# Receptances, output bias and low parts between an MLP and a block-wise mixture of experts: what moves to another engine or another place in the order

## The reference

```python
k = einsum('btd,ed->bte', x * tmk + xs * (1 - tmk), Wk) + bk
v = einsum('btd,ed->bte', x * tmv + xs * (1 - tmv), Wv) + bv
r = einsum('btd,ed->bte', silu(x * tmr + xs * (1 - tmr)), Wr) + br
# scan over t: a = e1 * a + e2 * v, b = e1 * b + e2, wkv = a / b
return einsum('btd,ed->bte', wkv * r, Wo) + bo
```

```python
topw, topi = top_k(softmax(x @ gate_w), 4)      # per token
out = sum over chosen experts of topw * (silu(x @ wg) * (x @ wu)) @ wd
out = out + sigmoid(x @ seg) * ((silu(x @ sg) * (x @ su)) @ sd)
```

## Time and profile before

| | us |
|---|---|
| runs, median (lowest to highest) of 3 | 564.64 (560.38 to 565.92) |
| the profiled execution's own time | 565.75 |
| its span, first to last instruction | 563.9 |
| busy: TensorE, VectorE, ScalarE, POOL | 436.9, 356.6, 271.6, 226.7 |
| TensorE's granted clock, mean over the span (1 is 2.4 GHz) | 0.871 |

### The profile page before, as it was taken

How to read it: one execution, slowest core, us unless ns; L and a number is a source line. 1 busy time by engine, 2 the same in 40 slices (tenths; PEclk the granted TensorE clock), 3 DMA queues, 4 the chain that set the end, 5 groups by cost and what they waited for, 6 DMA issues and landing times.

```text
span 563.9 us, 9855 instructions
## 1 busy us (share of the span) xinstructions
PE 436.9 (77%) x3348; PEld 303.8 (54%) x3348; DVE 356.6 (63%) x858; ACT 271.6 (48%) x518; POOL 226.7 (40%) x301
## 2 busy tenths in 40 slices
PE   1856799999997759788888152497879799999844
PEld 1634455555553348676777141376658566666433
DVE  5595458878873254946548989688673355555336
ACT  7314757767778424141683154352352355655402
POOL 5870224434566430601310254226627135565600
PEclk9956669999999779989799666678989999999958
DMA  7482071111330029600000000299902245444282
GB/s 215 140 147 96 23 99 45 36 36 45 118 102 7 1 80 331 200 1 1 1 1 1 28 28 28 82 230 244 301 29 99 80 111 148 135 140 117 64 309 77
DMA packets 52032, 56.02 MB, mean 99 GB/s; under 512 B 10244, under 2 KB 42893, under 8 KB 51984
## 3 DMA queue, kind: packets, MB, share of 16 engines
q1 hardware_dynamic: 47536, 46.67, 31.1%
q0 software_dynamic: 4448, 8.73, 4.6%
HBM read 35.61 MB, written 21.73 MB: 102 GB/s over the span
## 4 chain that ended last, share of the span: by engine, by line
PE 51%; DVE 22%; ACT 8%; issue 7%; POOL 4%; DMA 4%; SPq 2%; DVEq 0%; ACTq 0%; POOLq 0%
PE ps L2234 7%; PE ps L1971 5%; PE ps L1950 4%; PE ps L2021 4%; PE ps L1929 4%; PE ps L2257 4%; PE ps L2009 3%; PE ps L2215 3%; PE ps L2010 3%; PE ps L2011 3%; PE ps L1983 2%; DVE st L935 2%; ACT probs L1619 2%; DVE h_lo L1102 1%; PE ps L2349 1%
## 5 line engine op out<-in xcount | busy, mean ns | idle before, releaser
L1619 ACT ACTIVATE probs<-ps 128x512 f32<-128x512 f32 x160 | 87.0, 598 | 42.1 <-PE ps L1950 41.4
L1035 DVE TENSOR_REDUCE negm<-ps 128x2 f32<-128x1024 f32 (+1 forms) x64 | 67.6, 1082 | 16.6 <-PE ps L1939 16.1
L843 POOL DMA_INDIRECT y_slots_scratch<-yblk,ids x48 | 47.0, 979 | 50.0 <-issue 29.5
L677 POOL TENSOR_TENSOR rstd<-ve,halfneg 128x4 f32<-128x4 f32 x15 | 16.2, 1079 | 112.5 <-DVE ve L964 46.9
L1929 PE MATMUL ps<-k_all,q_ring 64*128 64x512 f32 (+3 forms) x256 | 51.9, 412 | 7.0 <-DVE negm L1035 4.2
L1971 PE MATMUL ps<-probs,v_all 128*32 128x128 f32 (+3 forms) x512 | 50.9, 474 | 4.8 <-DVE att L1063 3.2
L1950 PE MATMUL ps<-q_ring,k_all 64*128 64x512 f32 (+3 forms) x256 | 42.8, 392 | 14.8 <-ACT probs L1619 13.2
L1659 ACT CAST h_hi<-hf 128x512 fp32r<-128x512 f32 x28 | 17.4, 620 | 65.7 <-DVE hf L1093 63.5
L1950 PEld LDWEIGHTS ps<-q_ring,k_all 64*128 64x128 f32 x256 | 22.4, 201 | 48.7 <-ACT probs L1619 37.6
L1434 DVE COPY xcol<-ps 128x256 f32<-128x256 f32 x48 | 20.4, 424 | 39.2 <-PE ps L2215 39.2
L1038 DVE TENSOR_REDUCE negm<-ps 128x4 f32<-128x1024 f32 (+1 forms) x32 | 30.6, 959 | 21.2 <-PE ps L1939 21.2
(11 more groups left out here) (327 smaller groups left out, 1339.2 us busy)
## 6 DMA issues: line engine op xcount, KB each, us to landing
x_sorted_scratch<-pad SPq DMA_DIRECT2D x6, 1072.0 KB, 12.3
xblk<-x_sorted_scratch SPq DMA_DIRECT2D x96, 67.0 KB
wgu<-in_moe_w SPq DMA_DIRECT2D x4, 1536.0 KB, 17.5
q_ring<-q_parts_scratch SPq DMA_DIRECT2D x64, 64.0 KB
ycomb<-y_slots_scratch SPq DMA_DIRECT2D x8, 512.0 KB, 6.6
wd<-in_moe_w SPq DMA_DIRECT2D x1, 3072.0 KB, 18.4
sraw<-in_moe_w SPq DMA_DIRECT2D x6, 384.0 KB, 3.1
q_parts_scratch<-qparts SPq DMA_DIRECT2D x4, 512.0 KB, 4.5
```

Source lines behind the costliest of these rows:

```text
L843: pool.indirect_dma_start(out=y_slots, out_offset=bass.IndirectOffsetOnAxis(ap=ids[:, i:i + 1], axis=0), in_=yblk[:, i % YR, :], in_offset ...
L1035: dve.tensor_reduce(negm[:, par, :, hp, qt], pair_of, AX.X, ALU.max, negate=True).then_inc(s1_read, 1)
L1619: act.activation(probs[:, par, u, :], ps[:, col_unit(g, u), :], ACT.Exp)\
```

## The change

- VectorE's step 4 for batch 0 (two halves) becomes POOL's `wkv_low`, in POOL's queue behind `chunk_low(0)` and behind the second half of the mixes' low parts; `chunk_low(1)` moves behind the third. As `den` is now read by POOL, step 0 of batch 1 waits for `wkv_lo` ahead of writing it.
- The output bias is no longer added by VectorE: `mix_out` begins with two products of a row of ones and `bo` on TensorE, one for each PSUM bank, and its other products add to them. `out_stats` and `out_apply` read PSUM in place of `rows`.
- `receptances(1)` goes ahead of the wait for batch 0's rows and of their transposes.
- The shift of batch 0's rows goes behind the second reciprocal of `scan(1, 0, ...)`.
- Batch 1's rows: `in_apply` becomes `in_shift`, two tiles on VectorE (`in_half`) and two on ScalarE (`apply_rows(1, 2)`).
- On VectorE units 1 to 5 of the shared expert are split into gate and low part, with other work between; on TensorE `logits_of(1)` goes ahead of `shared_down(3)`, `ranks(1)` ahead of `shared_down(4)`.
- On POOL power 12 goes ahead of `scatter(0)`, and `scatter(1)` behind power 13.
- The wait for `zs_done` moves from ahead of the first block to the first block's down product.

```diff
+        def wkv_low(eng, b, m):
+            eng.wait_ge(wkv_hi, 2 * b + m + 1)
+            eng.tensor_tensor(cols_lo[:, m, b * T:(b + 1) * T], den[:, m, :],
+                              cols_hi[:, m, b * T:(b + 1) * T].bitcast(F32),
+                              ALU.subtract).then_inc(wkv_lo, 1)
...
             chunk_low(0)
+            wkv_low(pool, 0, 0)
             mix_low(1, 0)
             mix_low(1, 1)
+            wkv_low(pool, 0, 1)
+            mix_low(1, 2)
             chunk_low(1)
-            mix_low(1, 2)
             power(10)
             chunk_low(2)
             power(11)
...
+            power(12)
             scatter(0)
-            power(12)
-            scatter(1)
             power(13)
-            for u in range(2, TILES):
+            for u in range(1, TILES):
                 scatter(u)
...
-                if part == 2:
-                    for pair in range(2):
-                        dve.tensor_tensor(
-                            rows[:, b * TPB + 2 * pair:b * TPB + 2 * pair + 2, 0:D],
-                            ps[:, z_bank(part, b) + pair, :].rearrange("p (t d) -> p t d", t=2),
-                            bo_sb[:, :].unsqueeze(1).to_broadcast((P, 2, D)), ALU.add)\
-                            .then_inc(z_biased, 1)
-                    dve.wait_ge(z_biased, 2 * b + 2)
-                    statistics(b, lambda t: rows[:, b * TPB + t, 0:D])
-                else:
-                    statistics(b, lambda t: z_tile(part, b, t))
+                statistics(b, lambda t: z_tile(part, b, t))
...
+            def in_half(b):
+                dve.wait_ge(nmr_ready, b + 1)
+                for t in range(b * TPB, b * TPB + TPB // 2):
+                    dve.tensor_scalar(rows[:, t, 0:D], xb[:, t, :], rstd[:, t:t + 1],
+                                      nmr[:, t:t + 1], ALU.mult, ALU.add).then_inc(rows_ready, 1)
...
+                    if b >= 1:
+                        dve.wait_ge(wkv_lo, DC * (b - 1) + m + 1)
...
             scan(0, 1, 1)
-            scan(0, 0, 4)
...
             read_keys(1)
-            scan(0, 1, 4)
             mixes(1, 2)
...
             scan(1, 0, 1)
+            scan(1, 0, 2)
             in_shift(2, 0)
-            scan(1, 0, 2)
             scan(1, 0, 3)
...
             out_stats(2, 1)
-            shared_unit(1)
+            shared_gate(1)
             out_apply(2, 1)
-            shared_unit(2)
-            in_apply(2, 1)
-            shared_unit(3)
+            shared_low(1)
+            shared_gate(2)
+            in_shift(2, 1)
+            in_half(1)
+            shared_low(2)
+            shared_gate(3)
             split_low(3, 1)
+            shared_low(3)
             route_weights(0)
-            shared_unit(4)
+            shared_gate(4)
             route_top(1)
-            shared_unit(5)
+            shared_low(4)
+            shared_gate(5)
+            shared_low(5)
             route_places(1)
...
-            apply_rows(0)
+            apply_rows(0, 0)
...
             shared_unit(2)
+            apply_rows(1, TPB // 2)
             shared_unit(3)
...
             def mix_out(b):
+                pe.wait_ge(s_tail, 48)
+                for pair in range(2):
+                    pe.wait_ge(wkv_done, DC * b + pair + 1)
+                    pe.matmul(ps[:, z_bank(2, b) + pair, :].rearrange("p (t d) -> p t d", d=D),
+                              ones[0:1, :], bo_sb[0:1, :].unsqueeze(1).to_broadcast((1, 2, D)),
+                              start=True, stop=False, skip_group_check=True)
...
-                                       start=k == 0 and n == 0 and t % 2 == 0,
+                                       start=False,
...
                 pe.wait_ge(bh_copied, i + 1)
+                if i == 0:
+                    pe.wait_ge(zs_done, TILES)
...
             values(1)
+            receptances(1)
             pe.wait_ge(rows_ready, 5 * TPB)
             transposes(3, 0, rows_tile(0))
-            receptances(1)
             logits_of(0)
...
             shared_up(4)
+            logits_of(1)
             shared_down(3)
-            logits_of(1)
             logit_rows(1)
             shared_up(5)
+            ranks(1)
             shared_down(4)
-            ranks(1)
             shared_down(5)
...
             pe.wait_ge(s_wgu, 64)
-            pe.wait_ge(zs_done, TILES)
```

More of the change, by code:

```diff
@@ L358, in sandwich_kernel @@
         wkv_lo = sem("wkv_lo_ready")
-        z_biased = sem("z_biased")
         logit_cols = sem("routing_logits_as_columns")
@@ L981, in out_apply @@
                 for t in range(b * TPB, (b + 1) * TPB):
-                    z = (rows[:, t, 0:D] if part == 2
-                         else z_tile(part, b, t - b * TPB))
-                    dve.scalar_tensor_tensor(new[:, t, :], z, rstd[:, t:t + 1], old[:, t, :],
+                    dve.scalar_tensor_tensor(new[:, t, :], z_tile(part, b, t - b * TPB), rstd[:, t:t + 1], old[:, t, :],
                                              ALU.mult, ALU.add).then_inc(z_read, 1)
@@ L1157, in scan @@
                 else:
[L1158 to L1161, removed]
+                    wkv_low(dve, b, m)
             def start_columns(b):
@@ L1750, in route, with apply_rows @@
                 act.activation(wtop[:, h, :], wtop[:, h, :], ACT.Exp).then_inc(route_exp, 1)
-            def apply_rows(b):
-                act.wait_ge(nmr_ready, 1)
-                for t in range(b * TPB, (b + 1) * TPB):
+            def apply_rows(b, first):
+                act.wait_ge(nmr_ready, b + 1)
+                for t in range(b * TPB + first, (b + 1) * TPB):
                     act.activation(rows[:, t, 0:D], xb[:, t, :], ACT.Identity,
```

## The result

| | before | after |
|---|---|---|
| median of 20 runs each on one chip, us | 565.53 | 561.66 |
| lowest to highest | 560.38 to 568.06 | 557.97 to 567.2 |
| the profiled execution's own time | 565.75 | 558.38 |
| its span | 563.9 | 556.4 |
| granted clock, mean over the span | 0.871 | 0.879 |

The ratio is 0.9937, with an interval of 0.9912 to 0.9963: 3.6 us less, 2.1 to 5.0. The forecast was 5.8 less, to 558.8; the change came out faster by under 1%. 561.66 lies inside the stated range of 554.5 to 563.0, but outside the forecast's own range of 556.5 to 561, and nearer to the figures of three rivals (561.2, 561.2 and 561.3). Some 0.9 of the difference is the base: the forecast subtracted from 564.64, and the kernel before came out at 565.53.

What follows compares the result with a forecast made beforehand. VectorE set the pace where TensorE idled 15.0 us; from 352 to 367 the two waited for each other in turn. Leads 3.4 + 2.1 + 0.3 = 5.8 gave a median of 558.8 us, range 554.5 to 563.0.

Steps and rivals of the forecast that it cites:

- three rivals: Shared read path at 561.2, blocks' rows as bound at 561.2, order of units bringing nothing at 561.3; chances 0.12, 0.1, 0.06.
- The knot: Batch 0's rows, transposes, batch 1's receptances, reciprocals, low parts: logits start at 362.1 instead of 366.61; lead 4.5, then 3.5.
- Routing and residual: Routing to batch 1's residual: additions of 1.28 go, power comes before the scatter; lead grows from 3.5 to 6.7.
- Low parts to POOL: Two subtractions leave VectorE, freeing 0.6; stalls beside POOL bounded at 0 to 1.25 and taken as nothing.
- The rival of the read path: Moved subtractions stall the row shift (1.25) and one scan or the residual's shift (1.2) more: 561.2; chance 0.12.
- Bias on TensorE: Bias products in the output product take 1.9 a batch; batch 0 loses 0.2 at most, batch 1 nothing while covered.
- Statistics of batch 0: Two additions of 1.29 go; lead at the reciprocal of 352.96 taken as 0.3, bounded by a 0.9 stall.
- TensorE behind it: Behind batch 1's residual, unit 1's low part makes TensorE idle 384.0 to 387.3; lead 3.3 at batch 1's transposes.
- 1.7 lost: After TensorE's gap at unit 1's low part, part of the following products run at the low clock, costing 1.7.
- Blocks: Wait for the shared expert's scaled rows moves to the first down product: 2.1, plus 0.3; bounds 0 to 2.4.
- the order of the units brings nothing: Unit 1's low part keeps only its 1.2 lead up to the destinations, blocks add 2.1: 561.3; chance 0.06.
- The clock: Rival: TensorE's shorter bursts from 345 to 388 run at 1.2 GHz, making the kernel slower, up to 571.3; chance 0.06.

Runs made afterwards that it cites:

- e11: Combined version e8 with the output bias back on VectorE as in the kernel before; 558.02 us, ratio 0.9891 to the kernel before.
- e1: Changed kernel with the bias product over 128 rows (identity as weights) instead of one row; ratio 0.9958 to the kernel before.
- e8: Changed kernel plus the edits of e1, e4, e7 and unit 1's low part ahead of batch 1's residual; 555.17 us, ratio 0.9827 to the kernel before.
- e7: Changed kernel with weight chunk 2's low part behind power 11 on POOL instead of ahead; ratio 0.9892 to the kernel before.
- e4: Changed kernel with the low part of batch 0's first half back from POOL on VectorE; ratio 0.9887 to the kernel before.

## Why the prediction was right or wrong

**The knot: right.** Between the residual of batch 0 and the low parts the lead was to grow by 4.2 (0.3 to 4.5); it grew by 4.3 (-1.8 to 2.5). The logits were to give back 1.0 and gave 1.0. That they pay for coming after idle time is seen at 360.09, 0.61 with 0.43 behind it.

**Routing and residual: right.** The lead was to grow by 3.2 up to batch 1's residual (3.5 to 6.7); it grew by 3.2 (1.5 to 4.7). The power did come directly behind its variance. Of the two causes, e11 shows the additions (1.3); the order on POOL is read from the trace alone, as no run takes it back.

**Low parts to POOL: the step "I take nothing" failed.** The row shift ended with POOL's chunk, as said; but then POOL's new subtraction went ahead of the first row application, and held it until its own end. Price 0.9, inside the bounds of 0 to 1.25. The rival of the read path had this mechanism with other victims. In the section Who interferes with whom of SBUF — State Buffer the Trainium skill also names `tensor_scalar` among the operations that can take the pair of ports shared with GpSimd, when their operands meet the conditions of a mode, and the row application is a `tensor_scalar`: the trace agrees, with 2.28 for the four rows against 1.38. The prediction had drawn on its sentence about two SBUF inputs only.

**Bias on TensorE: the term was right in duration, wrong in "0.2 lost at most".** It took 1.98 for the 1.9. But it took the clock with it: behind it 15 of 24 products took 0.41 instead of 0.28, and `mix_out(0)` ended 2.4 later. 1.9 of that is the clock (e1); the other 0.5 goes with the late rows (20.82 in e1, 20.32 in e8). The prediction's argument about the clock knew only idle time as its cause. Batch 1's bias took the same 1.98 under the cover that the sum gave it, and cost nothing there.

**Statistics of batch 0: the bounds failed.** The stall was bounded at 0.9; the scan lost 1.55 to chunk 2's low part (e7). The mechanism was named, its size too small: in the trace of before POOL's subtraction had 0.89 left when the scan began (346.04 to 346.93), after the change 1.68 (341.14 to 342.82). With these three the residual was 1.8 late where it was to be 0.3 early: the 2.1 that every later row lacks.

**TensorE behind it: right in kind, the clock term under-sized.** From the residual's lead to unit 1's low part 5.5 were to be given back, measured 5.8. The gap was to be 3.3 and was 3.38. "1.7 lost" at the low clock was 2.5 (e4); so the lead at the transposes was 0.2, not 3.3: 2.1 from ahead of the knot, 0.3 from the residual, 0.8 from the clock. Behind them the two small steps came as forecast: the lead grew by 0.8 up to the routing of batch 1 (0.7) and lost 0.7 up to the destinations (0.6).

**Blocks: right, a little small,** 3.3 for 2.4.

In sum: 5.8 less 2.1, 0.3 and 0.8, plus 0.9, is 3.5; the trace shows 3.4 and the ratio of the runs 3.6. That the sum still fell inside the stated range owes something to its width and to the 0.9 that the blocks gave beyond their term, not to the terms that failed, which all erred the same way. None of the rivals came as written, though 561.66 lies near the figures of three; the nearest are the shared read path, with other victims, and "the order of the units brings nothing", whose place was right: there the lead went, but for another reason than the one given. The clock did not make it slower; its share was 1.9 ahead of the knot and 2.5 behind the gap, of which 1.7 were in the sum.

## What to carry to other kernels

Work that leaves a busy engine has to be looked at in the place where it lands: here a subtraction of 1.26 us on an idle POOL held up VectorE by 0.9, and the place of the next ones chose which VectorE instruction would stand (a scan, a variance or a row shift); beside the reciprocals of e7 one cost nothing. When a gain is followed from event to event, ask at each of them which engine then waits for an instruction that was put behind it: one low part put behind a residual cost nearly as much as the knot had brought. And compare traces from the last event that the change leaves alone, since what is the same in all these kernels differed by up to 5.6 us ahead of it (314.63 to 320.26).

## What was not expected of the hardware

Products that use one row of the array could be followed by 1.2 GHz although TensorE never stopped: behind batch 0's bias it was busy for 3.50 of 3.50 us at a granted clock of 0.51, against 1.00 behind the same number of columns in 128 rows. Over both batches of all these kernels that came in nine of twelve places with one row and in none of six with 128. What exactly the chip looks at, and why three places were spared, isn't shown by these runs. And a stretch at the low clock is dear or cheap by its place: the same 6.8 us cost 2.5 behind unit 1's low part and 0.8 in e4, where they fell on `mix_out(1)` and filled a gap.
